# A state-space scan on one Trainium2 core: step size transposed and multiplied by x in token layout, three steps scaled on GpSimd by one broadcast product, and the norm's shift made on GpSimd

## The reference, cut to what matters

```python
A = -exp(A_log)                                   # (256, 16)
x_dbl = einsum('bld,ed->ble', x, W_xproj)
dt_low, Bm, Cm = x_dbl[..., :64], x_dbl[..., 64:80], x_dbl[..., 80:]
delta = softplus(einsum('blr,dr->bld', dt_low, W_dt) + b_dt)
dA  = exp(delta[..., None] * A)
dBx = (delta * x)[..., None] * Bm[:, :, None, :]
# over the 128 tokens of a sequence:
h = dA_t * h + dBx_t
y = einsum('bdn,bn->bd', h, C_t)
x = layernorm(x + y)
```

## Time and profile before

| | before |
|---|---|
| median of 3 runs | 1335.4 us (1329.38 to 1335.6) |
| the profiled execution | 1339.98 us, its span 1338.2 us |
| first scan to last `hc` of the scan phase | 27.84 to 466.93 us of the span |
| TensorE clock granted, mean | 0.904 of full speed |

### The profile page before, as it was taken

The page is one execution under the profiler, slowest core; times in us unless marked ns, Lnnn a source line. Parts: engine busy times, 40 slices in busy tenths (PEclk is TensorE's granted clock), DMA queues, the critical chain, the costliest instruction groups (busy, mean ns, idle before and its releaser), DMA issues. The chain is left out here.

```text
span 1338.2 us, 28802 instructions
## 1 busy us (share of the span) xinstructions
PE 1039.9 (78%) x9883; PEld 874.9 (65%) x9883; DVE 914.6 (68%) x1657; ACT 806.0 (60%) x1817; POOL 868.6 (65%) x822
## 2 busy tenths in 40 slices
PE   5877777777877748888888886037999999999970
PEld 3766565666666636666666664036998998999960
DVE  2889889888798837777777783783555555555434
ACT  4988797887978436666666663123455555554433
POOL 1999999989999836777777773314253473354333
PEclk8898899988889869999999995558999999999995
DMA  3222322223222110111111100104233444343227
GB/s 119 86 90 79 98 88 83 89 72 95 90 82 72 56 30 30 37 38 45 36 36 40 43 26 26 71 1 138 67 97 68 112 96 103 71 96 80 32 24 259
DMA packets 61795, 97.01 MB, mean 72 GB/s; under 512 B 10305, under 2 KB 36514, under 8 KB 59682
## 3 DMA queue, kind: packets, MB, share of 16 engines
q1 hardware_dynamic: 49442, 79.12, 18.2%
q0 software_dynamic: 12288, 17.05, 7.7%
HBM read 74.74 MB, written 21.40 MB: 72 GB/s over the span
## 5 line engine op out<-in xcount | busy, mean ns | idle before, releaser
L455 DVE TENSOR_TENSOR_SCAN scan_state<-scan_decay,scan_drive_ps 128x512 f32<-128x512 f32 x256 | 295.0, 1200 | 47.3 <-PE scan_drive_ps L281 35.3
L541 POOL TENSOR_TENSOR scan_hc<-scan_state,scan_c_sb 128x1024 f32<-128x1024 f32 x128 | 299.3, 2372 | 22.5 <-PE scan_drive_ps L281 16.4
L281 PE MATMUL scan_drive_ps<-all_ident,scan_scaled 128*128 128x128 f32 x1024 | 178.9, 303 | 102.0 <-DVE scan_state L455 59.8
L1595 POOL DMA_INDIRECT acc<-expert_rows,input_lst x64 | 111.3, 1739 | 182.0 <-DVE expert_rows L1724 167.3
L281 PEld LDWEIGHTS scan_drive_ps<-all_ident,scan_scaled 128*128 128x128 f32 x1024 | 126.3, 153 | 148.4 <-DVE scan_state L455 92.3
L1698 DVE TENSOR_TENSOR expert_hid_lo<-expert_hid,expert_hid_hi 128x512 fp32r<-128x512 f32 x128 | 88.6, 692 | 172.4 <-ACT expert_hid_hi L1682 172.4
L1677 ACT ACTIVATE expert_hid<-expert_h_ps,expert_b 128x512 f32<-128x512 f32 x128 | 88.1, 689 | 189.8 <-PE expert_h_ps L565 187.4
L376 ACT ACTIVATE scan_decay<-scan_delta,scan_a_neg 128x508 f32<-128x508 f32 x256 | 168.2, 710 | 12.8 <-DVE scan_state L455 12.8
L292 PE MATMUL scan_y_ps<-all_ident,scan_hc 128*128 128x128 f32 x1024 | 164.7, 288 | 2.6 <-POOL scan_hc L541 2.4
L386 ACT ACTIVATE scan_scaled<-scan_dxT,scan_bT 128x256 f32<-128x256 f32 x384 | 162.7, 498 | 0.0
L563 PE MATMUL expert_o_ps<-weights_w_hi,expert_hid_hi 128*128 128x256 f32 x512 | 143.3, 280 | 3.3 <-DVE expert_hid_lo L1698 3.3
(11 more groups left out here) (207 smaller groups left out, 2408.4 us busy)
## 6 DMA issues: line engine op xcount, KB each, us to landing
scan_c_sb<-rows SPq DMA_DIRECT2D x128, 256.0 KB, 3.1
weights_w<-w SPq DMA_DIRECT2D x16, 1024.0 KB, 4.9
table<-all_row SPq DMA_DIRECT2D x32, 132.0 KB, 1.8
scan_xT<-xT SPq DMA_DIRECT2D x8, 512.0 KB, 4.4
attn_ctxT<-ctxT SPq DMA_DIRECT2D x32, 128.0 KB, 2.5
acc<-all_row SPq DMA_DIRECT2D x32, 128.0 KB, 1.7
final_a<-acc SPq DMA_DIRECT2D x8, 512.0 KB, 7.4
out<-final_o SPq DMA_DIRECT2D x8, 512.0 KB, 4.1
```

Of the source, the lines that this page charges most:

```text
L281: last = pe.transpose(drive_ps[k][:, j * P:(j + 1) * P], scaled[:, p.slot, j, k * P:(k + 1) * P], ident[0][:])
L455: dve.tensor_tensor_scan(state[:, p.slot, k, :], decay[:, p.slot, k, :, :].rearrange("p b t -> p (b t)"), drive_ps[k][:], 0.0, ALU.mult, A ...
L541: pool.tensor_tensor(hc[:, p.slot, :, :], state[:, p.slot, :, :], c_sb[:, p.slot, :].unsqueeze(1).broadcast_to([P, KH, GT]), ALU.mult).the ...
L1595: pool.indirect_dma_start(out=acc_dram, out_offset=bass.IndirectOffsetOnAxis(ap=lst[h.parity][:, n:n + 1], axis=0), in_=rows[h.part][:, t, ...
```

## The change

It has four parts. `dx` is gone: PE transposes `delta` itself (`turn_delta`), and DVE multiplies the transposed halves in PSUM by `x_tok`, x in token layout, straight into `dxT` at step 13. `x_tok` is a new input that SP loads by one more DMA of 512 KB for each group, behind that of `xT`. ACT's copies to `dxT` are gone. POOL scales in steps 4, 9 and 14 in place of 3, 7, 11 and 15, by one product of 128x1024 with the column of `bT` broadcast, and ACT scales the other thirteen. And `shift` is made on POOL by two products in a row, between `outputs` of steps 4 and 5, with `rstd` one step earlier on ACT.

```diff
-POOL_STEPS = (3, 7, 11, 15)
+POOL_STEPS = (4, 9, 14)
...
-                    sp.wait_ge(dx_ready, grp.g - 1)
+                    sp.wait_ge(dxT_ready, 2 * (grp.g - 1))
                     sp.sem_inc(x_free, 1)
                     sp.dma_start(xT[grp.par][:], xT_dram[:, :, ds(grp.g * GT, GT)]).then_inc(x_loaded[grp.par], 16)
+                    sp.dma_start(x_tok[grp.par][:], x_dram[:, ds(grp.g * GB, GB), :]).then_inc(x_tok_loaded[grp.par], 16)
...
-                def turn_dx(grp, half):
-                    pe.wait_ge(dx_ready, grp.g + 1)
+                def turn_delta(grp, half):
+                    pe.wait_ge(delta_ready, KH * (grp.g + 1))
...
-                            last = pe.transpose(m_ps[half][:, c:c + P], dx[:, k, b * P:(b + 1) * P], ident[0][:])
-                    last.then_inc(dx_turned, 1)
+                            last = pe.transpose(m_ps[half][:, c:c + P], delta[grp.par][:, k, b, :], ident[0][:])
+                    last.then_inc(delta_turned, 1)
...
-                    if n == 13:
-                        copy_dx(grp, 0)
-                        copy_dx(grp, 1)
...
-                            if n == 6:
+                            if n == 5:
                                 inv_std(grp.minus_one())
...
-                def step_inputs(grp):
-                    dve.wait_ge(delta_ready, KH * (grp.g + 1))
-                    since(dve, dx_turned, 2 * grp.g)
-                    dve.tensor_tensor(dx[:], delta[grp.par][:].rearrange("p k b t -> p k (b t)"), xT[grp.par][:], ALU.mult).then_inc(dx_ready, 1)
+                def step_inputs(grp, half):
+
+                    dve.wait_ge(delta_turned, 2 * grp.g + half + 1)
...
+                    dve.tensor_tensor(dxT[grp.par][:, 2 * half:2 * half + 2, :].rearrange("p j d -> p (j d)"), m_ps[half][:],
+                                      x_tok[grp.par][:, 2 * half:2 * half + 2, :].rearrange("p j d -> p (j d)"), ALU.mult).then_inc(dxT_ready, 1)
...
-                    if (n, half) == (12, 0):
-                        step_inputs(grp)
+                    if n == 13:
+                        step_inputs(grp, half)
...
-                                if (n, half) == (6, 1):
-                                    shifts(grp.minus_one())
...
-                    for j in range(GB):
-                        last = pool.tensor_scalar(scaled[:, p.slot, j, :], dxT[p.par][:, j, :], bT[p.par][:, j, p.n:p.n + 1], None, ALU.mult)
-                    last.then_inc(scaled_by_pool, 1)
+                    pool.tensor_tensor(scaled[:, p.slot, :, :], dxT[p.par][:], bT[p.par][:, :, p.n:p.n + 1].broadcast_to([P, GB, D]),
+                                       ALU.mult).then_inc(scaled_by_pool, 1)
+
+                def shifts(grp):
+                    pool.wait_ge(rstd_ready, grp.g + 1)
+                    pool.sem_inc(rstd_seen, 1)
+                    pool.tensor_tensor(mean_std[:], moment[:, :, 0], rstd[:], ALU.mult).then_inc(mean_std_ready, 1)
+                    pool.wait_ge(mean_std_ready, grp.g + 1)
+                    since(pool, normed, grp.g)
+                    pool.sem_inc(mean_std_seen, 1)
+                    pool.tensor_tensor(shift[:], zero[:], mean_std[:], ALU.subtract).then_inc(shift_ready, 1)
...
+                        if n == 5 and grp.at(n - STEPS) is not None:
+                            shifts(grp.minus_one())
                         outputs(grp.at(n))
```

More of the change, by code:

```diff
@@ L113, in scan_phase @@
         delta = [s.sb(f"delta{i}", [P, KH, GB, SEQ]) for i in range(2)]
-        dx = s.sb("dx", [P, KH, GT])
+        x_tok = [s.sb(f"x_tok{i}", [P, GB, D]) for i in range(2)]
         dxT = [s.sb(f"dxT{i}", [P, GB, D]) for i in range(2)]
@@ L123, in scan_phase @@
         moment = s.sb("moment", [P, GB, 2])
+        mean_std = s.sb("mean_std", [P, GB])
+        zero = s.sb("zero", [P, GB])
         shift = s.sb("shift", [P, GB])
@@ L149, in scan_phase @@
         delta_ready = s.sem("delta_ready")
-        dx_ready = s.sem("dx_ready")
-        dx_turned = s.sem("dx_turned")
+        x_tok_loaded = [s.sem(f"x_tok_loaded{i}") for i in range(2)]
+        delta_turned = s.sem("delta_turned")
         dxT_ready = s.sem("dxT_ready")
@@ L166, in scan_phase @@
         normed = s.sem("normed")
+        mean_std_ready = s.sem("mean_std_ready")
+        mean_std_seen = s.sem("mean_std_seen")
+        rstd_seen = s.sem("rstd_seen")
         stats_seen = s.sem("stats_seen")
@@ L217, in _ @@
                 sp.dma_start(a_log[:], a_log_dram).then_inc(const_loaded, 16)
+                sp.dma_start(x_tok[0][:], x_dram[:, 0:GB, :]).then_inc(x_tok_loaded[0], 16)
                 sp.dma_start(xT[1][:], xT_dram[:, :, GT:2 * GT]).then_inc(x_loaded[1], 16)
+                sp.dma_start(x_tok[1][:], x_dram[:, GB:2 * GB, :]).then_inc(x_tok_loaded[1], 16)
                 store_c(Group(0, 0))
@@ L309, in prepare @@
                     if n == 12:
-                        turn_dx(grp, half)
+                        turn_delta(grp, half)
                 def group(grp):
@@ L364, in softplus_log @@
                     act.activation(z_log[:], z_exp[:], ACT.Ln, bias=1.0).then_inc(z_log_ready, 1)
[L366 to L369, removed]
                 def decays(p):
@@ L462, in step_sizes @@
                                              ALU.max, ALU.add).then_inc(delta_ready, 1)
[L464 to L467 removed]
+                def step_inputs(grp, half):
+                    dve.wait_ge(delta_turned, 2 * grp.g + half + 1)
+                    if half == 0:
+                        dve.wait_ge(x_tok_loaded[grp.par], 16 * (grp.pair + 1))
+                        since(dve, scaled_by_pool, len(POOL_STEPS) * (grp.g - 1))
+                        since(dve, scaled_by_act, len(ACT_STEPS) * (grp.g - 1))
+                    dve.tensor_tensor(dxT[grp.par][:, 2 * half:2 * half + 2, :].rearrange("p j d -> p (j d)"), m_ps[half][:],
+                                      x_tok[grp.par][:, 2 * half:2 * half + 2, :].rearrange("p j d -> p (j d)"), ALU.mult).then_inc(dxT_ready, 1)
                 def statistics(grp, half):
@@ L481, in aggregate @@
                     last.then_inc(mv_ready, 1)
[L483 to L486, removed]
                 def prepare(grp, n, half):
@@ L1842, in _, with build @@
                     last.then_inc(normed_pool, 1)
-def build(nc, xT, w_proj, w_dt, a_log, ident_dram, ctxT, w_q, w_kv, w_o, w_g, norm, even_odd, pick,
+def build(nc, xT, x_tok, w_proj, w_dt, a_log, ident_dram, ctxT, w_q, w_kv, w_o, w_g, norm, even_odd, pick,
           bits_i, bits_f, same, before, iota, place, w1, b1, w2, b2, out):
@@ L1860, in build @@
             attention = AttentionConstants(Scope(nc, front, "xattn"), w_q, w_kv, w_o, w_g, norm, even_odd, pick)
-            scanned = scan_phase(nc, x1, (ident, ident_dram), xT, w_proj, w_dt, a_log, rows, attention)
+            scanned = scan_phase(nc, x1, (ident, ident_dram), xT, x_tok, w_proj, w_dt, a_log, rows, attention)
             attention_phase(nc, x1, ident, gate_all, attention, ctxT, table, acc, choice, row, row_stored, scanned)
@@ L1900 @@
         "xT": halves(x.reshape(T, D).T),
+        "x_tok": np.ascontiguousarray(x.reshape(NT, P, D).transpose(1, 0, 2)),
         "w_proj": halves(w_xproj.T),
```

5 lines of the change are left out of this document (3 added, 2 removed).

## The result

| | before | after |
|---|---|---|
| median | 1332.39 us (1328.72 to 1335.6, 4 runs) | 1292.13 us (1287.02 to 1294.32, 4 runs) |
| ratio | | 0.9693 [0.9649, 0.9737] |
| profiled execution, its span | 1339.98, 1338.2 us | 1294.32, 1292.5 us |
| first scan | 27.84 us | 25.56 us |
| last group's normalisation starts | 473.82 us | 407.61 us |

The kernel became 40 us faster. The scan phase gave 66.2 us, and the attention phase, whose code the change does not touch, took 19.9 back: -66.2 + 19.9 + 0.6 = -45.7, the difference of the spans. The medians differ by 40.3 us: the profiled execution of before was 7.6 us above the median in this table, that of after 2.2 us above its own.

The account below looks back on a forecast made before the run. POOL, busy 52.54 of 55.2 us a group, was taken as the bound, with ACT next at 46.5. Start, first steps, six groups, end and last shift summed to -61.7 on 1340.0, 1278; at the median 1275, range 1263 to 1302.

Parts of the forecast that it names:

- ACT 46.5 becomes the bound: Scan phase, one group: ACT scales one more step, loses two copies, and at 46.5 us becomes the fullest engine.
- The group then costs 47.3: Scan phase, one group: ACT's 46.5, 0.5 of waiting for dxT and 0.3 of other idle time make 47.3 us.
- I take 2.33: POOL's scaling: one broadcast product costs 2.33 us, like an hc; upper bound 3.6.
- The small products, 0.5: POOL's two products for shift, with two hand-overs between engines: 0.5 us a group, bounds 0.3 and 1.0.
- (a): New wait in the scan loop: ACT waits for dxT at the next group's step 0, 0 to 0.5 us, taken as 0.5.
- (b): New wait in the scan loop: POOL waits for rstd ahead of step 5's hc, taken as nothing.
- (c): Scan phase's loads: x_tok's load lies in the queue ahead of the next broadcasts of C, taken as hidden.
- The start, -2.1: Start of the scan phase: delta and dxT are ready earlier, -2.1 us, bounds -2.1 and +2.6.
- Together -61.7: Sum over the scan phase's stretches and the last shift: 61.7 us less on a profiled execution of 1340.0.
- The change is confined to the scan phase: Opening step: only the scan phase, 27.84 to 466.93 us, is read as affected by the change.
- Rival 1: Scan loop: mutual waits of ACT and POOL give a period of 49 to 52 us, 1295 us; chance 0.25.
- Rivals 2 and 3: POOL's product far dearer, 1360 us, chance 0.03; the gap only moves to POOL's rstd wait, 1330 to 1338, chance 0.03.

Follow-up runs that it names:

- e9: After plus eight tiny memsets of an unused tile at VectorE's start, so its attention loop begins behind instruction 524: 1273.35 us, ratio 0.9559 to before.
- e4: After with POOL scaling four steps (3, 7, 11, 15), still by one product each: 1280.48 us, ratio 0.9588 to before.
- e10: Before plus three tiny memsets at VectorE's start, so its attention loop begins behind instruction 516: 1351.05 us, ratio 1.0144 to before.
- e2: Before with only POOL's four steps scaled by one broadcast product each: 1275.36 us, ratio 0.9554 to before.
- e1: Before with only shift moved to POOL and rstd a step earlier: 1325.20 us, ratio 0.9938 to before.
- e3: Before with only dxT made by DVE from the transposed delta and x_tok: 1329.31 us, ratio 0.9977 to before.
- e5: After with shift back on DVE after step 6 and rstd back at step 6: 1274.11 us, ratio 0.9545 to before.

## Why the prediction was right, and where it was wrong

1275 us, range 1263 to 1302, was forecast; it came to 1292. The range held it, but the 17 us between do not come from the scan phase. With the attention phase undisturbed the whole change takes 1273 us (e9): the mechanism of the scan phase was right. That 1292 lay in the range was in part luck: the forecast by itself ended at 1289, and the range went on to 1302 for a rival that did not come true.

- "ACT 46.5 becomes the bound": 46.1, and shown by e4.
- "The group then costs 47.3": 47.1.
- POOL's product "I take 2.33": 1.91. A term mis-sized, and below the lower bound, which was `hc` itself. POOL came to 43.4 us for 44.8. Since ACT is the bound, it moved the period little; POOL idles 3.7 us a group, where the forecast left it 2.5.
- The small products, 0.5: 0.6. (a) ACT's wait for `dxT`, 0.5: 0.8. (b) nothing for `rstd`: right but for the last group. (c) the load hidden: right for the broadcasts of C, for which nobody waits in the loop. PE waits for `xT` in six groups now, 6.7 us in all, where before it did once, but PE is not the bound.
- DVE 40.5: 40.5. The start, -2.1: -2.3.
- "Together -61.7", of which -62.2 up to the last `hc`: it ended at 401.1 for 466.9 us, 65.9 earlier, and the last normalisation came 66.2 us earlier. Cut at the shifts, the start gave 2.3, the way to the first `shift` 8.2, six groups 48.7 and the end 7.1. So some 4 us are more than forecast, most of them outside the six groups. That the cheaper product did it there, where POOL has more weight, is a guess.
- **The step that failed** stands at the beginning: "The change is confined to the scan phase". The sum carried the rest of the span over unchanged. The change moved VectorE's attention loop from behind instruction 513 of its queue to behind 516, and that phase lost 19.9 us, nearly all to a lower clock. Neither a term nor a rival held it; what the runs showed is the loss by place (e9, e10).
- Rival 1 gave 1295 us, the nearest number, by mutual waits and a period of 49 to 52. The period is 47.1 and POOL never stands for `rstd` within the loop: its mechanism is refuted, and its number was met by luck. Rivals 2 and 3 are refuted by the product's 1.91 us and by the period.

What the forecast overlooked in its own favour as well: nearly all of the gain is one edit. e2 alone is as fast as e9, the whole change with the attention phase undisturbed (1275.4 and 1273.4 us); e1 and e3 alone give 0.6% and nothing that can be told from no change.

## What to carry to other kernels

- Before moving work between engines, ask what one instruction of the full engine costs in another form: a broadcast product in place of four column scalings gave 83% of the period's gain, and set a new split (four steps on POOL, not three).
- A stand behind a full engine is worth its time only while that engine is the bound. `shift` lasted 6 us in before and cost 2.1 us a group there (e1), and it cost nothing once POOL had 4.0 us of idle time a group in short gaps (e5).
- When a phase that was not edited changes its time, compare it between the two traces by itself. If its instructions are the same and only an "issue" stand and the clock differ, shift the code by a few idle instructions before explaining anything else.

## What the runs showed of the hardware that was not expected

- The place of a loop in VectorE's queue changes its time. Behind 505, 513 and 524 the attention phase takes 359.0 to 360.1 us in nine kernels, behind 516 it takes 370.8 to 379.0 in five, with one stand of 0.36 to 0.38 us without a releaser and then about 0.12 us more in every second sequence, at the same instruction. The Trainium skill (Runtime: NRT & Kernel Launch, "Instruction fetch mechanics") has the sequencer fetch in blocks of 256 instructions, and a taken branch out of the two present blocks stall. As an estimate from that page, a loop of 67 instructions lies in at most two such blocks wherever it begins, and the loops behind 505, 513, 516 and 524 would behave alike; the runs show that they do not. What tells them apart is open, and so is whether it has to do with the fetch at all.
- In before TensorE's clock stays at full (2.4 GHz) for 310.6 us, in after it falls to half (1.2 GHz) for 6.8 us six times in the same code, and each fall costs 3.0 us. That VectorE's small stands tip it is argued: in the loop it falls in none of the nine kernels without them, and in each of the five with them a stand came ahead of the first fall. It was not tried by itself, and a stand is not enough: PE stood for 1.13 us ahead of the fall at 602.6 us in after and for 0.98 us without one in before, but also for 1.12 us without one in e10, at 611.3 us.
- GpSimd's product of 128x1024 with one operand a broadcast column takes 1.91 us, where the same operation with an operand repeated once (`hc`) takes 2.37 and four scalings by a column of 128x256 take 3.70.
